# A neighbourhood attention kernel on one core: the values' stationary operand with 4 columns of ones rather than 32

## The reference

```python
x = x + conv3x3(gn(x), W)                    # 32 groups of 4 channels
x = x + attention(gn(x), w_qkv, b_qkv, rpb, w_proj, b_proj)

# attention: 16 heads of 8 channels; every position sees a 7x7 window, clipped at the image's edge
logits = einsum(q, k_window) + rpb[relative row, relative column]     # 49 per position and head
out    = sum(softmax(logits) * v_window)
return out @ w_proj + b_proj
```

## Time and profile before

| | |
|---|---|
| median of 3 runs | 1427.41 us |
| lowest, highest | 1421.59, 1437.48 us |
| the profiled execution | 1432.87 us |
| its span (first to last instruction) | 1431.1 us |
| TensorE's mean granted clock in it | 0.859 of full speed |

### The profile page before, as it was taken

The page is one execution under the profiler, slowest core; times in us unless marked ns, Lnnn a source line. Parts: engine busy times, 40 slices in busy tenths (PEclk is TensorE's granted clock), DMA queues, the critical chain, the costliest instruction groups (busy, mean ns, idle before and its releaser), DMA issues.

```text
span 1431.1 us, 38250 instructions
## 1 busy us (share of the span) xinstructions
PE 1158.9 (81%) x12441; PEld 811.7 (57%) x12441; DVE 880.3 (62%) x2129; ACT 674.5 (47%) x1867; POOL 593.9 (42%) x1278
## 2 busy tenths in 40 slices
PE   3799998556888788778979887888789788879882
PEld 3455555444666556556656664666556566656661
DVE  3422222696777576667757674767577676757671
ACT  2100000703565556565746655565557465655651
POOL 3000000500746455454636462646455454637461
PEclk7799999556899897889989997999888889989996
DMA  9200000241547374645555464657375554645472
GB/s 253 56 35 34 34 34 34 74 99 20 144 103 177 80 179 104 140 113 125 144 107 142 101 161 76 156 100 171 82 181 127 113 141 96 157 98 144 98 179 51
DMA packets 142497, 159.57 MB, mean 112 GB/s; under 512 B 29952, under 2 KB 119888, under 8 KB 142040
## 3 DMA queue, kind: packets, MB, share of 16 engines
q1 hardware_dynamic: 141432, 153.13, 45.3%
q0 software_dynamic: 864, 3.90, 0.8%
HBM read 86.09 MB, written 70.47 MB: 109 GB/s over the span
## 4 chain that ended last, share of the span: by engine, by line
PE 53%; DMA 26%; DVE 9%; issue 6%; SPq 4%; ACT 0%; POOL 0%; DVEq 0%; POOLq 0%; ACTq 0%
DMA area<-mcol 22%; PE PS L1080 13%; PE PS L1185 11%; PE PS L1148 9%; PE PS L1169 5%; PE PS L1092 4%; PE PS L1162 3%; DVE bias L933 3%; PE PS L1133 3%; PE PS L1195 3%; DVE area L975 2%; DMA area<-x 2%; SPq L423 1%; SPq L444 1%; DVE mcol L986 1%
## 5 line engine op out<-in xcount | busy, mean ns | idle before, releaser
L570 POOL TENSOR_TENSOR halves<-masked 128x96 f32<-128x96 f32 (+1 forms) x512 | 203.5, 397 | 493.3 <-DVE masked L1007 492.7
L1148 PE MATMUL PS<-area 97*128 97x48 bf16 (+1 forms) x4112 | 257.8, 211 | 138.9 <-DMA area<-mcol 119.7
L996 DVE TENSOR_TENSOR S<-PS,bias 128x384 f32<-128x384 f32 (+1 forms) x513 | 283.9, 554 | 121.2 <-PE PS L1148 115.9
L746 ACT ACTIVATE VT<-PS 128x128 f32<-128x128 f32 x449 | 126.2, 281 | 418.2 <-PE PS L1133 416.0
L1185 PE MATMUL PS<-S,VT 128*64 128x96 f32 (+1 forms) x4096 | 310.5, 278 | 0.0
L1148 PEld LDWEIGHTS PS<-area 97*128 97x128 bf16 x4112 | 186.6, 105 | 217.2 <-issue 158.9
L753 ACT ACTIVATE S<-S 128x384 f32<-128x384 f32 (+1 forms) x512 | 274.7, 539 | 46.5 <-DVE S L996 33.3
L1185 PEld LDWEIGHTS PS<-S,VT 128*64 128x64 f32 x4096 | 207.1, 148 | 143.5 <-issue 91.7
L1007 DVE TENSOR_TENSOR masked<-PS,cst 128x192 f32<-128x192 f32 (+1 forms) x512 | 181.6, 355 | 101.2 <-PE PS L1185 95.2
L986 DVE TENSOR_REDUCE mcol<-PS 128x6 bf16<-128x480 f32 (+2 forms) x297 | 181.5, 611 | 96.2 <-PE PS L1169 96.1
L1080 PE MATMUL PS<-area 128*128 128x392 f32 x576 | 192.0, 496 | 3.9 <-DVE area L875 3.9
(11 more groups left out here) (87 smaller groups left out, 1142.3 us busy)
## 6 DMA issues: line engine op xcount, KB each, us to landing
k_parts<-area SPq DMA_DIRECT2D x204, 168.0 KB, 4.1
area<-k_parts SPq DMA_DIRECT2D x33, 1008.0 KB, 8.3
q_parts<-area SPq DMA_DIRECT2D x204, 98.0 KB, 2.3
area<-q_parts SPq DMA_DIRECT2D x66, 294.0 KB, 5.9
xa<-x_mid SPq DMA_DIRECT2D x18, 392.0 KB, 6.6
late<-x_mid SPq DMA_DIRECT2D x17, 392.0 KB, 8.8
out<-area SPq DMA_DIRECT2D x17, 392.0 KB, 8.5
den<-sums SPq DMA_DIRECT2D x66, 98.0 KB
```

The source lines that it names most:

```text
L570: nc.gpsimd.tensor_tensor(h, m[:, :, 0:2, :], m[:, :, 2:4, :], ALU.add).then_inc(s["half"], 1)
L996: nc.vector.tensor_tensor(S[:, n % 4, 0:cols], PS[:, SCORE + n % 2, 0:cols], bias[:, at:at + cols], ALU.add).then_inc(s["biased"], 1)
L1148: last = mm(PS[:, SCORE + n % 2, cols * g:cols * (g + 1)], key_rows[a][0:PEAK_ROW + 1, g, key:key + 128], query_rows[a][0:PEAK_ROW + 1, g, ...
```

## The change

VT has 36 columns for each group, 32 of values and 4 of ones, instead of 64. Each `weigh` matmul so writes partitions 0 to 35 or 64 to 99. The mask gives row 32+h of a half the head h; before, rows 32 to 63 had their head by p % 32 // 8, the same as the values' rows. The collection of the sums reads partitions 32 to 35 and 96 to 99 instead of every eighth from 32 to 63 and from 96 to 127. The partitions 36 to 63 and 100 to 127 of the two banks are no longer written by `weigh` but still read by `select_heads`, so both banks are cleared once, where there was a memset of one element.

```diff
+VALUE_COLS = 32 + 4
...
-    c[:, C_OUT:C_OUT + 4] = p[:, None] % 32 // HEAD_DIM == np.arange(4)[None]
+    own = np.where(p % 64 < 32, p % 32 // HEAD_DIM, p % 64 - 32)
+    c[:, C_OUT:C_OUT + 4] = own[:, None] == np.arange(4)[None]
...
-        VT = sb("VT", [128, 4, 4, 64])
+        VT = sb("VT", [128, 4, 4, VALUE_COLS])
...
-                                 sel[64 * g + 32:64 * g + 64:HEAD_DIM, (c + 1) % 2, :, :, :].rearrange("p g q t -> p (g q t)")
+                                 sel[64 * g + 32:64 * g + VALUE_COLS, (c + 1) % 2, :, :, :].rearrange("p g q t -> p (g q t)")
...
-            nc.vector.memset(small[:, 2, 0:1], 0.0).then_inc(s["init"], 1)
+            nc.vector.memset(PS[:, SUM:SUM + 2, :], 0.0).then_inc(s["init"], 1)
...
-                    last = mm(PS[64 * (g % 2):64 * (g % 2) + 64, SUM + n % 2, at:at + q], VT[:, w % 4, g, :],
+                    last = mm(PS[64 * (g % 2):64 * (g % 2) + VALUE_COLS, SUM + n % 2, at:at + q], VT[:, w % 4, g, :],
                               S[:, n % 4, q * g:q * (g + 1)], start=True, stop=True)
```

## The result

The changed kernel takes 1419.57 us at the median of 18 runs (1412.20 to 1429.12), the kernel before 1426.88 us over as many on the same chip (1420.15 to 1437.48). The ratio is 0.9936, with a 95% interval of 0.9911 to 0.9961: 9.1 us faster, between 5.6 and 12.7. This is the ratio of the means, 1419.24 and 1428.39 us; the medians alone are 7.3 us apart, inside the interval. On a second chip the two gave 0.9934 (0.9909 to 0.9958). The profiled execution took 1416.90 us, its span is 1415.1 us and its mean granted clock 0.849.

What follows compares the result with a forecast made beforehand. Each chunk was taken as TensorE's pace up to the reciprocal, then a fixed transfer chain of some 14 us. Loads -5.4, memset +1.0 and collection +1.0 gave -3.4 us: 1424.0 us, range 1413 to 1434.

Steps and rivals of the forecast that it cites:

- 24 ns on each tile's first load, at either clock: In each tile's first pair of value matmuls: 28 columns fewer at 0.86 ns save 24 ns, at full or half clock.
- the load term: Shorter first weight loads in the 8 tiles a chunk from the maxima's arrival to the reciprocal: 5.4 us saved in all.
- nothing in the four that the queue sets: In four of sixteen odd chunks the sync queue is later than VectorE's reciprocal, so shorter loads save nothing there.
- the slack of 0.31 us: In odd chunks the sync queue's last store ends 0.31 us before the reciprocals' store is issued, covering the 0.19 us gain.
- 0 to +0.3 us: Price of collecting sums from neighbouring partitions, in the sync queue; taken at 0.15 us, together +1.0 us in odd chunks.
- The memset, +1.03 us: At the kernel's start, clearing 128x1024 in PSUM takes 1.09 us instead of 0.06, with nothing hiding it.
- no gain from the load: Rival: the load does not shrink or nobody waits for it, leaving 1428.4 to 1429.6 us; chance 0.15.
- the whole gain arrives: Rival: five more tiles a chunk count, 3.8 us, and the collection is free: -8.2 us, 1419; chance 0.10.
- neither clock case: Rivals on TensorE's granted clock: worse, 1436 to 1444 us, chance 0.12; better, 1416 to 1420 us, chance 0.15.
- the split pairs: Rival: 36 columns make each value matmul run alone on the array, 82 us more, 1506; chance 0.02.
- Two signs of being wrong: Prediction wrong if time from reciprocal to next chunk's first scores moves, or mean granted clock moves by over 0.01.
- The wait for the maxima: TensorE's wait for the small DMA bringing the maxima, once a chunk, would grow by 0.1 to 0.2 us each.

Runs made afterwards that it cites:

- the experiment with the columns alone: The changed kernel with collection and mask as in the kernel before, so 36 columns but the old partitions read: ratio 0.9944 to the kernel before, 8.0 us faster.

## Why the prediction was right, and where it was off

The forecast was 1424.0 us, -3.4 us; it is -9.1 us. The mechanism held: the pairs stay pairs at a pace of 0.08 us, only the first pair's load is exposed, and that load carries the gain. Its size did not: the gain is 2.7 times the forecast, and the result lies in the range of 1413 to 1434 because that range was kept wide for the clock and the unknown costs. The sizes of all three terms were off, and one had the wrong sign.

*"24 ns on each tile's first load, at either clock".* This is the miss that the traces show best. At the full clock it is 23 to 24 ns. At half clock it is 46 to 47 (215.0 to 168.4). I had concluded from an equal exposure of 0.05 us at both clocks to an equal price per column, but an exposed remainder says nothing of the slope. The longest record of a load, 232 ns, stood in the earlier trace rows and would have told: 100 ns more than the shortest for the same 64 columns. A quarter to a little over a third of the tiles that count run at half clock. With that, and with all 32 chunks instead of 28, the load term is 7.7 us instead of 5.4.

*"nothing in the four that the queue sets", and the slack of 0.31 us.* I read the slack from the end of the last store to L481 and did not ask what the stores themselves wait for. In 14 of the 16 odd chunks of the kernel before they wait for GpSimd, which follows TensorE, so there the queue gains what TensorE gains. In the four late chunks something else came on top: in three of them one store's long issue, 1.35 us in that of the earlier trace rows, and in the fourth a collection that took 3.58 us instead of 2.45. That the saving arrives in these four too is counted into the 7.7 us but not shown.

*The collection, "0 to +0.3 us", taken at +0.15.* It has the other sign. I priced the packets and put the issue at nothing ("bytes, rows and issues are the same"). The packets did get slower, but the issue of each of the two DMAs fell from 0.63 to 0.29 us. So the term is not +1.0 us but -0.6, the time at the very end, and whatever arrives in late chunks, which no run could tell from nothing: 0.9944 without the cheap collection and 0.9936 with it have intervals that overlap.

*The memset, +1.03 us,* is +0.85: 0.912 us for 1024 elements, not 1.09. Four times the 0.272 us of 256 elements counts four times the fixed part, and the earlier trace rows had that part too, 0.059 us with one element: 0.059 + 4 x (0.272 - 0.059) = 0.911 us. The fill of PSUM has the pace of that of SBUF.

The sum by what was measured is -7.7 + 0.85 - 0.6 = -7.5 us, within the interval of -5.6 to -12.7; the 1.6 us up to the measured 9.1 are within the noise and have no named cause.

Of the rivals: no gain from the load is out; "the whole gain arrives" gave 1419, close to the result, by five more tiles a chunk (3.8 us) and a free collection. The collection is indeed not a cost, and whether those tiles count stays open, since just 3.8 us are left between the means from reciprocal to gate; neither clock case is needed, since the mean clock of the timed runs hardly differs (0.849 and 0.848 in the experiment with the columns alone); the split pairs did not come. Two signs of being wrong that the prediction named came up in the first pair of profiles: the time from reciprocal to gate moved by 10.3 us, and the clock by 0.0107 (0.8593 to 0.8486). Kernels that all load 64 columns for the first pair spread just as far, 506.1 to 514.3 us and 0.844 to 0.859, so as signs for one execution they were too sharp. The wait for the maxima was to grow by 0.1 to 0.2 us a gate and did not show it in one profile (115.2 us in 34 waits, 3.4 us each, before 3.6): the scatter of the landings is larger.

## What to carry to other kernels

Where small groups of matmuls on halves of the array stand between matmuls on the whole of it, look at the start of the second pair: here the group's first weight load stood bare, and it was paid by the column. So pad the stationary operand no further than the result needs, and put the narrow operands first. An exposed remainder that is the same under two conditions doesn't show that the price behind it is; compare whole records at either level of the clock. And before calling a queue late or early by its last instruction, look at what the instructions ahead of it wait for, and count it in more than one profile.

## What the runs showed of the hardware

- A load of f32 weights takes 0.82 ns a column at the full clock and 1.71 at half (64, 48 and 36 columns: the shortest 132, 119, 109 ns, the longest 232, 204, 184). The exposed part of the first load is 51, 38, 27 ns and 55, 28, 8 ns.
- Operands of 36 and 48 columns run in pairs on the two halves of the array at the pace of 64: 82.5 ns a pair of 96 moving f32 columns at the full clock, 160 at half.
- A DMA from four partitions to HBM is issued in 0.286 us when the partitions are neighbours and in 0.63 when they are 2 or 8 apart. Its four packets of 3136 B take 121 to 129 ns each 8 apart, 176 at the median and up to 316 as neighbours.
- A fill of PSUM by VectorE takes 0.912 us for 128x1024 and 0.485 for 128x512 f32, that is 0.83 ns an element and 0.06 us; one of SBUF 0.272 for 128x256, which is the same pace.
